# Attention states stored by strips of two heads, late results in the attention weights' banks, dense operands moved to 128 bytes past a multiple of 512

## The chip, the cores and the metric

The kernel runs on one core of one Trainium2 chip. The metric is the device time in microseconds of one execution. Three executions of the kernel before took 1625.15, 1625.56 and 1628.57 us, median 1625.56.

## The reference

The input is x, 8 rows of 512 tokens of 512 numbers, float32. Cut to what matters:

```python
xn = layernorm(x)                                  # no weights
# attention layer s(xn): a gated recurrence over tokens, 16 heads, keys of 16, values of 32
a  = rmsnorm(xn, ln1_w)
q, k, v, g = a @ Wq, a @ Wk * 32**-0.5, a @ Wv, a @ Wg + bg
gk = log_sigmoid(a @ Wkg1 @ Wkg2 + bkg2) / 16      # rank 16 inside
S  = S * exp(gk_t)[..., None] + k_t[..., None] * v_t[..., None, :]   # per head, 16 x 32
o_t = q_t @ S
o  = silu(g) * normalised_per_head(o)
x1 = xn + o @ Wo
s  = x1 + (silu(rmsnorm(x1, ln2_w) @ W1) * (rmsnorm(x1, ln2_w) @ W3)) @ W2   # hidden 1408
# the other branch: 8 low-rank experts mixed by a softmax, rank 64
g2 = silu(sum_k alpha_k * U_k @ (V_k @ xn)),  alpha = softmax(relu(xn @ fW1 + b1) @ fW2 + b2)
out = x + s * g2
```

## The kernel before

Every large product is made in float32r from operands split into a high and a low part: three matmuls (hi·hi, hi·lo or lo·hi, and the third) into one PSUM bank (`product3`, lines 153 to 163). A plain float32 matmul shows as two records in the trace.

There are three stages, one after the other, each a loop over the 8 rows (counted from 0 here): `phase_f` (names f_, the layer norm, the experts and the gate), `phase_a` (names a_, attention) and `phase_m` (names m_, the MLP and the output). At each seam work of the next stage is put into the last row of the one before: `Lent` gives attention's first keys, queries and gates banks of the f stage, and `Front` in `phase_m` gives the MLP's first three hidden blocks (of 128) the dense banks of attention's last row.

The order of the work is written out by hand for each engine (`sync`, `vector`, `gpsimd`, `scalar`, `tensor` in each stage), with semaphores counted through `Counts`. `loop_parts` runs a body per row and, inside it, named parts of the row ahead. A class `Regions` is a ring of PSUM places: results take them in turn in a fixed order, and `free`, `ready` and `taken` are the waits for a place empty, filled and read.

A row of attention, on PE: for each of 4 chunks of 128 tokens, the masked attention weights within the chunk (`weights`, L1282: 64 products on 32x32 tiles, heads' pairs on four strips of 32 partitions, each strip in a bank of its own), the turned keys (L1366, two transposes), a part of the next row (k0 and k1, the inner gate u, q0, q1), the variance of the chunk before (L1303), the product of the carried state with the queries (L1390), the state's addition (`state_products`, L1351) and the weighted values (L1399, 16 heads, 128x32 tiles). Then the key gates z, the values v0 to v3, the output gates g0 to g3 and the output products o0 to o3. The state has for each of two groups of 8 heads 128 partitions (8 heads of 16 keys) by 256 columns (8 heads of 32 values), with zeros outside each head's block, made on DVE with `hmask` (L1031) and decayed on L1043. ACT reads the mix (L1216 square, L1219 copy, after DVE's L1063 of the chunk before), the turned keys (L1203), q and k (L1129), and v (L1149). The inner gate is copied on DVE in four steps (L931 to L935). DVE clears the attention weights' banks once (`clear_weights`, L1012), since the upper halves of blocks are never written.

Of the 8 banks attention has four `a_ps` (three for the dense ring, one for the mix) and four for the attention weights. An MLP row is 11 blocks: `up_products` (L1529 to L1531, 2 x 12 matmuls, stationary operand m_w, moving m_xs) and `down` (L1543 to L1545, 12 matmuls, moving m_h). Block j uses tile m_w`j`.

Tensors in SBUF stand in the order of their allocation, each rounded up to 32 bytes. In the built program the constants begin at byte 16512 of a partition and row0 at 19136. Counting on from there: a_wkhi to a_wolo begin 192 past a multiple of 512, all dense tensors of the f stage and a_xa begin 128 past one, a_og and a_v_tok 192, m_w0 to m_w4 192 (they take the place of the attention weights), m_w5 to m_w10, m_xs and m_h 128.

## Time and profile before

| | |
|---|---|
| median of 3 runs | 1625.56 us (1625.15 to 1628.57) |
| the profiled execution | 1622.4 us |
| its span, first to last instruction | 1620.7 us |
| mean granted clock of TensorE | 0.998 |
| PE busy | 1593.2 us, 98% |
| PE weight loads | 1277.6 us, 79% |
| DVE, ACT, POOL busy | 847.3, 567.2, 167.2 us |

The f stage ends at about 342 us, attention at 885 us, the MLP fills the rest. Busy time is that of the union of an engine's records. A matmul's record reaches from its start to its modelled end, over the start of the next, so neither the busy share of PE nor a matmul's mean says how fast matmuls follow each other. The start of one stretch in the timeline and the start of the next do.

### The profile page before, as it was taken

The numbers are of one execution on the slowest core, as the hardware profiler recorded it, in microseconds if no ns is written. First come the engines' busy times: TensorE is split into PE (matmuls) and PEld (weight loads), VectorE is DVE, ScalarE is ACT, GpSimd is POOL, SyncE is SP. The second block draws the span as 40 slices with busy tenths as digits, with TensorE's granted clock in tenths as the row PEclk, the third lists the DMA queues.
The fourth block names the chain that finished last, engine by engine and source line by source line (L and its number), as shares of the span: only waits on it lengthen the run. The fifth ranks groups of instructions, "written<-read, shape, count | busy, mean of one in ns | idle before, by whom it ended". The sixth has DMA issues, their size and how long they took to land.

```text
span 1620.7 us, 30581 instructions
## 1 busy us (share of the span) xinstructions
PE 1593.2 (98%) x12274; PEld 1277.6 (79%) x12274; DVE 847.3 (52%) x1311; ACT 567.2 (35%) x982; POOL 167.2 (10%) x190
## 2 busy tenths in 40 slices
PE   7999999999999999999999999999999999999998
PEld 5777888777777777777777788888888888888886
DVE  5565455367797887978876451331415142241413
ACT  4333343366564645636564411111111111111111
POOL 4770000100220102101020000000000000000000
PEclk9999999999999999999999999999999999999999
DMA  7563332101020210202213423030301203030200
GB/s 175 151 135 78 83 95 69 59 27 52 9 84 0 84 53 32 84 0 84 84 54 118 144 101 127 0 136 0 136 0 49 87 0 136 0 136 0 91 14 26
DMA packets 50700, 113.16 MB, mean 70 GB/s; under 512 B 13321, under 2 KB 24665, under 8 KB 42466
## 3 DMA queue, kind: packets, MB, share of 16 engines
q1 hardware_dynamic: 47906, 99.95, 19.5%
q10 hardware_dynamic: 1152, 8.39, 1.3%
q0 software_dynamic: 1600, 4.25, 0.9%
q8 instruction: 28, 0.46, 0.1%
q14 instruction: 14, 0.11, 0.0%
HBM read 78.98 MB, written 33.59 MB: 69 GB/s over the span
## 4 chain that ended last, share of the span: by engine, by line
PE 94%; DVE 2%; ACT 1%; issue 1%; DMA 1%; PEld 0%; SPq 0%; ACTq 0%; DVEq 0%; PEldq 0%
PE m_ps L1529 10%; PE m_ps L1531 10%; PE m_ps L1530 10%; PE a_ps L160 7%; PE a_ps L162 7%; PE a_ps L161 7%; PE f_ps L160 5%; PE f_ps L162 5%; PE f_ps L161 5%; PE m_ps L1543 5%; PE m_ps L1544 5%; PE m_ps L1545 5%; PE a_att L1282 3%; PE a_ps L1399 2%; PE a_ps L1303 2%; PE a_ps L1390 1%
## 5 line engine op out<-in xcount | busy, mean ns | idle before, releaser
L1529 PE MATMUL m_ps<-m_xshi,m_w 128*128 128x512 f32 x680 | 268.1, 394 | 1.4 <-DVE m_w L1520 1.4
L1766 DVE TENSOR_TENSOR m_h<-m_ps,m_silu 128x512 f32<-128x512 f32 x85 | 58.7, 690 | 402.4 <-PE m_ps L1531 402.4
L1531 PE MATMUL m_ps<-m_xshi,m_w 128*128 128x512 f32 x680 | 266.5, 392 | 0.0
L1530 PE MATMUL m_ps<-m_xslo,m_w 128*128 128x512 f32 x680 | 266.4, 392 | 0.0
L1830 ACT ACTIVATE m_silu<-m_ps 128x512 f32<-128x512 f32 x85 | 50.8, 597 | 334.3 <-PE m_ps L1531 334.3
L1529 PEld LDWEIGHTS m_ps<-m_xshi,m_w 128*128 128x128 f32 x680 | 127.7, 188 | 30.0 <-issue 2.1
L1531 PEld LDWEIGHTS m_ps<-m_xshi,m_w 128*128 128x128 f32 x680 | 127.6, 188 | 28.7
L1530 PEld LDWEIGHTS m_ps<-m_xslo,m_w 128*128 128x128 f32 x680 | 127.7, 188 | 28.1 <-issue 0.2
L1101 POOL TENSOR_TENSOR row<-row,a_r 128x512 f32<-128x512 f32 x32 | 50.7, 1615 | 331.6 <-DMA a_r<-scratch_r 331.6
L1022 DVE TENSOR_TENSOR a_a<-a_att,causal 128x1024 f32<-128x1024 f32 x64 | 75.2, 1216 | 11.8 <-PE a_att L1282 11.8
L1839 ACT ACTIVATE m_h0hi<-m_h 128x512 fp32r<-128x512 f32 x46 | 29.1, 632 | 135.7 <-DVE m_h L1766 135.7
L1543 PE MATMUL m_ps<-m_h0hi,m_w 128*128 128x512 f32 x192 | 75.3, 392 | 0.0
L1544 PE MATMUL m_ps<-m_h0lo,m_w 128*128 128x512 f32 x192 | 75.3, 392 | 0.0
L1545 PE MATMUL m_ps<-m_h0hi,m_w 128*128 128x512 f32 x192 | 75.3, 392 | 0.0
L1839 ACT ACTIVATE m_h1hi<-m_h 128x512 fp32r<-128x512 f32 x39 | 24.7, 632 | 115.6 <-DVE m_h L1766 115.6
L1107 POOL TENSOR_TENSOR a_cum<-a_cum 128x512 f32<-128x512 f32 x24 | 30.7, 1281 | 321.3 <-ACT a_cum L1190 321.3
L1543 PE MATMUL m_ps<-m_h1hi,m_w 128*128 128x512 f32 x160 | 62.6, 391 | 0.0
L1544 PE MATMUL m_ps<-m_h1lo,m_w 128*128 128x512 f32 x160 | 62.6, 391 | 0.0
L1545 PE MATMUL m_ps<-m_h1hi,m_w 128*128 128x512 f32 x160 | 62.6, 391 | 0.0
L160 PE MATMUL f_ps<-f_xnhi,f_w1hi 128*128 128x512 f32 x128 | 52.1, 407 | 2.5 <-DVE f_xnlo L476 1.2
L160 PE MATMUL a_ps<-a_wvhi,a_xahi 128*128 128x512 f32 x128 | 53.1, 415 | 0.0
L160 PE MATMUL a_ps<-a_xahi,a_wghi 128*128 128x512 f32 x128 | 50.8, 397 | 0.9 <-ACT a_v_tok L1149 0.6
(306 smaller groups left out, 3487.9 us busy)
## 6 DMA issues: line engine op xcount, KB each, us to landing
row<-scratch_xn SPq DMA_DIRECT2D x16, 1024.0 KB, 4.9
row<-scratch_xmid SPq DMA_DIRECT2D x16, 1024.0 KB, 7.3
m_xt<-in_L_attn_W SPq DMA_DIRECT2D x33, 256.0 KB, 3.2
f_xt<-in_L_attn_x SPq DMA_DIRECT2D x32, 256.0 KB, 8.1
scratch_xn<-row SPq DMA_DIRECT2D x8, 1024.0 KB, 9.0
scratch_gate<-row ACTq DMA_DIRECT2D x8, 1024.0 KB, 3.9
scratch_xmid<-row SPq DMA_DIRECT2D x8, 1024.0 KB, 3.9
row<-scratch_gate SPq DMA_DIRECT2D x8, 1024.0 KB, 10.5
```

Source lines behind the costliest of these rows:

```text
L160: pe.matmul(out, lh, rh, start=first and n == 0, stop=False)
L161: pe.matmul(out, lh, rl, start=False, stop=False)
L162: ins = pe.matmul(out, ll, rh, start=False, stop=last and n == end)
L1022: dve.tensor_tensor(a_sb[n].rearrange("p s g o t -> p (s g o) t"), ps, bcast(causal, 1, 4 * GR), ALU.mult).then_inc(att.taken_sem(f"{c}_{n ...
L1529: pe.matmul(ps, wh, xh, start=k == 0, stop=False)
L1530: pe.matmul(ps, wh, xl, start=False, stop=False)
L1531: ins = pe.matmul(ps, wl, xh, start=False, stop=k == LAST)
L1543: pe.matmul(ps, lh, rh, start=j == 0, stop=False)
L1544: pe.matmul(ps, lh, rl, start=False, stop=False)
L1545: ins = pe.matmul(ps, ll, rh, start=False, stop=j == FT - 1)
L1766: dve.tensor_tensor(h[n], dense.region(f"b{j}"), silu[n], ALU.mult).then_inc(dense.taken_sem(f"b{j}"), 1)
L1839: act.activation(h_hl[n][0], h[n], ACT.Copy).then_inc(count.sem("hhi"), 1)
```

## The change

- States: 128 partitions by 2 x 32 columns per group (a partition holds its head's values in one of two column halves, chosen by `parity`), not 256. One DVE operation makes both groups. The product with the queries is made by strips of 32 partitions (two heads), 64 output partitions each, eight per chunk.
- PSUM: two dense banks, two for the mix (even and odd quads of heads), and the attention weights' four banks take z0, z1, v1, v2, g0, g1, g2 as well. Places are given by a table in place of turns. The turned keys go to the second half of the mix's odd bank. `clear_weights` goes.
- Inner gate: the weights hold its 16 columns three times high and once low, so one ACT copy of 64 partitions and one DVE subtraction fill what four DVE operations did. Its matmuls have 64 and 48 columns in place of 48 and 16.
- SBUF: small tensors and a pad of 256 bytes go ahead of the attention weights, a pad of 448 bytes ahead of m_w0; decay and last stand behind a_v_tok.

The diff, cut to its core:

```diff
     def __init__(self, counts, name, regions, order, early=(), places=None):
...
-            r = n % len(regions)
+            r = places[result] if places else n % len(regions)
...
+    w = {name: sb(name, shape) for name, shape in (
+        ("bkg2", [P, KD // P]), ("bg", [P, KT]), ("ln1", [P, KT]), ("mean", [P, D // 32]),
+        ("ln2", [P, KT]), ("pad", [P, 64]))}
...
-    w["wkg1"] = sb("wkg1", [P, KT, 32 + RANK], F32R)
+    w["wkg1"] = sb("wkg1", [P, KT, 4 * RANK], F32R)
...
-        state = [sb(f"state{n}", [P, GR, HG * VH]) for n in range(2)]
+        state = [sb(f"state{n}", [P, GR, 2 * VH]) for n in range(2)]
...
-        psum = [ctx.enter_context(nc.psum_tensor(f"a_ps{b}", [P, 512], F32))[:] for b in range(4)]
+        psum = [ctx.enter_context(nc.psum_tensor(f"a_ps{b}", [P, 512], F32))[:] for b in range(2)]
+        ps_mix = ctx.enter_context(nc.psum_tensor("a_mix", [P, 2, 512], F32))[:]
+        EVEN, ODD = 0, 1
...
+        places = {result: n for n, results in enumerate((
+            ["k0", "ds0", "var0", "q0", "ds2", "var2", "var3", "v3", "o0", "o2"],
+            ["k1", "u", "ds1", "var1", "q1", "ms", "v0", "g3", "o1", "o3"],
+            ["z0", "g0"], ["z1", "g1"], ["v1", "g2"], ["v2"])) for result in results}
...
+        turned = Regions(count, "kt", [ps_mix[:, ODD, GR * P:]], list(range(NC - 1)))
-        mix = Regions(count, "mix", psum[3:4], list(range(NC)))
+        mix = Regions(count, "mix", [ps_mix[:, :, 0:QD // 2 * P]], list(range(NC)))
...
 # DVE, inner gate
-                dve.tensor_copy(u[0:RANK], ps).then_inc(count.sem("uhi"), 1)
-                dve.tensor_copy(u[64:64 + RANK], ps).then_inc(count.sem("uhi"), 1)
-                dve.tensor_copy(u[96:96 + RANK], at.region("u")[32:32 + RANK]).then_inc(count.sem("uhi"), 1)
                 dve.wait_ge(*count.at("uhi", i))
-                dve.tensor_tensor(u[32:32 + RANK], ps, u[0:RANK].bitcast(F32), ALU.subtract).then_inc(at.taken_sem("u"), 1)
+                dve.tensor_tensor(u[low], at.region("u")[low], u[low].bitcast(F32), ALU.subtract).then_inc(at.taken_sem("u"), 1)
 # DVE, state
-                        for g in range(GR):
-                            ins = dve.tensor_tensor(new[:, g, :].rearrange("p (h o v) -> p h o v", o=2, v=VH),
-                                                    bcast(ds[:, g], 1, HG // 2),
-                                                    bcast(hmask.rearrange("p (h o) -> p h o", o=2), 3, VH), ALU.mult)
+                        dve.tensor_tensor(new.rearrange("p g (o v) -> p g o v", v=VH), ds,
+                                          bcast(bcast(parity, 1, GR), 3, VH), ALU.mult).then_inc(dense.taken_sem(f"ds{c}"), 1)
 # ACT
+            def inner_gate(i, at=dense):
+                act.wait_ge(*at.ready("u", i))
+                act.activation(u[0:4 * RANK], at.region("u")[0:4 * RANK], ACT.Copy).then_inc(count.sem("uhi"), 1)
...
+                    if c == 0:
+                        keys(i, c)
+                    if c == 1:
+                        squares(i, (2,))
+                    for part in (("k0", "k1"), ("u",), ("q0",), ("q1",))[c]:
                         ahead(part)
+                    if 0 < c < NC - 1:
+                        keys(i, c)
 # PE
+                    for part in (("k0", "k1"), ("u",), ("q0",), ("q1",))[c]:
+                        ahead(part)
+                    if 0 < c < NC - 1:
+                        pe.wait_ge(*mix.taken(c - 1, i))
+                        turned_keys(i, c)
...
+                    if 0 < c < NC - 1:
+                        pe.wait_ge(*turned.taken(c, i))
...
-                        for quad in range(QD):
-                            g, first_head = quad * HQ // HG, quad * HQ % HG
-                            pe.matmul(ps[:, quad, :], state[c % 2][:, g, first_head * VH:(first_head + HQ) * VH],
-                                      qhat[:, gcs[g], :], start=quad == 0, stop=True, skip_group_check=True)
+                        for g in range(GR):
+                            for strip in range(4):
+                                rows, at = slice(H32 * strip, H32 * (strip + 1)), H64 * (strip % 2)
+                                pe.matmul(ps[2 * g + strip // 2][at:at + H64], state[c % 2][rows, g, :],
+                                          qhat[rows, gcs[g], :], start=g == 0, stop=True, skip_group_check=True,
+                                          tile_position=(H32 * strip, at))
...
+            parts["v0"](0)
+            for m in range(KT):
+                pe.wait_ge(*f.dense.taken(f"u{m}", NB - 1))
+            for part in ("v1", "g"):
                 parts[part](0)
+            pe.wait_ge(*dense.taken(f"g{LAST - 1}", 0))
...
+        sb("pad", [P, 112])
         w = [sb(f"w{j}", [P, 3, 2, KT, P], F32R) for j in range(5)]
```

## Rows read from the trace of the kernel before

**Rows 1.** the profile page, its head, busy times and clock in 40 slices.

```profile
span 1620.7 us, 30581 instructions
...
PE 1593.2 (98%) x12274; PEld 1277.6 (79%) x12274; DVE 847.3 (52%) x1311; ACT 567.2 (35%) x982; POOL 167.2 (10%) x190
...
PEclk9999999999999999999999999999999999999999
```

**Rows 2.** the list of what PE waited for: engine, line, releaser: us, times, longest.

```profile
PE a_ps L160 <- DVE a_xalo L923: 1.6, 1, 1.6
PE m_ps L1529 <- DVE m_w L1520: 1.4, 1, 1.4
```

**Rows 3.** timeline of PE, MLP row 1: start us, us, engine, line, out<-in, count.

```profile
983.29 0.40 PE L1529 MATMUL m_ps<-m_xshi,m_w 128*128 128x512 f32 x1
...
988.89 0.40 PE L1543 MATMUL m_ps<-m_h0hi,m_w 128*128 128x512 f32 x1
...
1024.71 0.39 PE L1529 MATMUL m_ps<-m_xshi,m_w 128*128 128x512 f32 x1
...
1030.15 0.39 PE L1543 MATMUL m_ps<-m_h1hi,m_w 128*128 128x512 f32 x1
```

**Rows 4.** timeline of PE, first and next-after matmul of four stretches of 48.

```profile
331.44 0.39 PE L160 MATMUL f_ps<-f_vxhi,f_uthi 128*128 128x512 f32 x1
...
342.33 0.40 PE L160 MATMUL a_ps<-a_wvhi,a_xahi 128*128 128x512 f32 x1
...
353.34 0.39 PE L160 MATMUL a_ps<-a_xahi,a_wghi 128*128 128x512 f32 x1
...
478.81 0.39 PE L160 MATMUL a_ps<-a_xahi,a_wghi 128*128 128x512 f32 x1
...
490.00 0.40 PE L160 MATMUL a_ps<-a_oghi,a_wohi 128*128 128x512 f32 x1
...
500.68 0.39 PE L162 MATMUL a_ps<-a_oghi,a_wolo 128*128 128x512 f32 x1
```

**Rows 5.** timeline of PE, attention row 2, chunk 1.

```profile
514.44 1.05 PE L1390 MATMUL a_ps<-a_neg,a_state 128*128 128x128 f32 x8
...
515.43 0.43 PE L1351 MATMUL a_ps<-a_v_tok,a_fold 128*32 128x64 f32 x16
...
515.67 0.52 PE L1399 MATMUL a_ps<-a_a,a_v_tok 128*32 128x128 f32 x12
...
516.66 0.33 PE L1282 MATMUL a_att<-a_qx,a_lv 32*32 32x128 f32 x6
...
518.29 0.33 PE L1366 MATMUL a_ps<-ident,a_soft 128*128 128x128 f32 x1
```

**Rows 6.** timeline of DVE, the same chunk; in brackets idle time before.

```profile
513.80 0.67 DVE L931 CAST a_u<-a_ps 16x512 fp32r<-16x512 f32 x1
...
516.64 0.76 DVE L1031 TENSOR_TENSOR a_state<-a_ps,hmask 128x256 f32<-128x256 f32 x2
...
518.50 0.69 DVE L1063 TENSOR_TENSOR a_rn<-a_rn,a_oc 128x512 f32<-128x512 f32 x1
```

**Rows 7.** timeline of attention row 0: PE's gates and outputs, DVE's last weighing.

```profile
411.33 0.50 PE L160 MATMUL a_ps<-a_xahi,a_wghi 128*128 128x512 f32 x1 [0.48 <-ACT a_v_tok L1149]
...
423.60 0.39 PE L160 MATMUL a_ps<-a_oghi,a_wohi 128*128 128x512 f32 x1
...
424.87 1.22 DVE L994 TENSOR_TENSOR a_neg<-a_neg,a_q 128x1024 f32<-128x1024 f32 x1
```

**Rows 8.** timeline of attention row 2, chunk 2: ACT, and PE's start of the variance.

```profile
519.23 0.60 ACT L1219 ACTIVATE a_oc<-a_ps 128x512 f32<-128x512 f32 x1 [1.83 <-DVE a_rn L1063]
...
519.72 0.38 ACT L1203 ACTIVATE a_fold<-a_ps 128x256 f32<-128x256 f32 x1
...
521.36 0.59 PE L1303 MATMUL a_ps<-a_sq,avg 128*128 128x512 f32 x1
...
521.56 0.60 ACT L1129 ACTIVATE a_q<-a_ps 128x512 f32<-128x512 f32 x1 [1.45 <-PE a_ps L162]
```

More of the change, by code:

```diff
@@ L269, in prepare_attention_weights @@
     step(pool.memset(w["wkg2"].bitcast(F32), 0.0))
-    step(pool.memset(w["wkg1"].bitcast(F32), 0.0))
     RANK, KD = Wkg2.shape
-    small = w["stage"][0:RANK, 1, 0:KD]
+    small = w["stage"][0:4 * RANK, 1, 0:KD]
     sources = {"wkg1": Wkg1, "wk": Wk, "wq": Wq, "wv": Wv, "wg": Wg, "wo": Wo}
@@ L795, in phase_a @@
         wkg1, wq, wk, wv, wg, wo = (w[name] for name in ("wkg1", "wq", "wk", "wv", "wg", "wo"))
-        RANK = wkg1.shape[2] - 32
+        RANK = wkg1.shape[2] // 4
         wkg2, bkg2_sb, bg_sb, ln1_sb = w["wkg2"], w["bkg2"], w["bg"], w["ln1"]
@@ L836, in phase_a @@
                           ("decay", 1), ("m64", 3), ("m32", 3), ("mdk", 1), ("mdq", 2), ("mkh", 1), ("mqh", 1),
-                          ("state", GR * (NC - 2)), ("first", NC - 1), ("weighing", NC),
+                          ("state", GR * (NC - 2)), ("weighing", NC),
                           ("sq", NC), ("rn", NC), ("og", 2 * NC), ("oghi", NC), ("oglo", NC)):
@@ L843, in phase_a @@
         assert GR == 2 and NC == 4
[L845 to L848 removed]
+        order = [("k0", ["k0"]), ("k1", ["k1"]), (None, ["ds0"]), ("u", ["u"]), (None, ["var0", "ds1"]),
+                 ("q0", ["q0"]), (None, ["var1", "ds2"]), ("q1", ["q1"]), (None, ["var2", "ms"]),
+                 ("z", zs), ("v0", values[:1]), (None, ["var3"]), ("v1", values[1:]), ("g", gates),
                  (None, outs), ("body", [])]
+        places = {result: n for n, results in enumerate((
+            ["k0", "ds0", "var0", "q0", "ds2", "var2", "var3", "v3", "o0", "o2"],
+            ["k1", "u", "ds1", "var1", "q1", "ms", "v0", "g3", "o1", "o3"],
+            ["z0", "g0"], ["z1", "g1"], ["v1", "g2"], ["v2"])) for result in results}
         early = {part: results for part, results in order if part}
[L851 to L852 removed]
+        dense = Regions(count, "dense", psum + [ps[:, strip].rearrange("p g o t -> p (g o t)") for ps in ps_att for strip in range(2)],
+                        sum((results for _, results in order), []), sum(early.values(), []), places)
+        turned = Regions(count, "kt", [ps_mix[:, ODD, GR * P:]], list(range(NC - 1)))
         att = Regions(count, "att", ps_att, [f"{c}_{n}" for c in range(NC) for n in range(2)])
[L854 removed]
+        mix = Regions(count, "mix", [ps_mix[:, :, 0:QD // 2 * P]], list(range(NC)))
         LAST = KT - 1
@@ L1005, in clear @@
                 dve.memset(u.bitcast(F32), 0.0)
-            def clear_weights():
-                for m in range(KT):
-                    dve.wait_ge(*f.dense.taken(f"u{m}", NB - 1))
-                for ps in ps_att:
-                    for strip in range(2):
-                        dve.memset(ps[:, strip], 0.0)
             def body(i, ahead):
@@ L1196, in deviation, with keys, by_quads @@
                 act.activation(added[0:1], added[0:1], ACT.Exp, scale=-0.5).then_inc(count.sem("r2"), 1)
+            def keys(i, c):
+                act.wait_ge(*turned.ready(c, i))
+                act.activation(flat(kt_sb), turned.region(c), ACT.Copy).then_inc(turned.taken_sem(c), 1)
+            def by_quads(ap):
+                return ap.rearrange("p (g b) t -> p g b t", b=2)
             def body(i, ahead):
@@ L1245, in first_row @@
                 elif part == "lent":
-                    for name in ("k0", "k1"):
+                    for name in ("u", "k0", "k1"):
                         parts[name](0, first)
@@ L1317, in inner_gate @@
                 for k in range(KT):
-                    pe.matmul(ps[0:32 + RANK], wkg1[:, k, :], xa_hl[0][:, k, :], start=k == 0, stop=False,
+                    pe.matmul(ps[0:4 * RANK], wkg1[:, k, :], xa_hl[0][:, k, :], start=k == 0, stop=False,
                               skip_group_check=True)
-                    ins = pe.matmul(ps[0:RANK], wkg1[:, k, 0:RANK], xa_hl[1][:, k, :], start=False, stop=k == LAST,
+                    ins = pe.matmul(ps[0:3 * RANK], wkg1[:, k, 0:3 * RANK], xa_hl[1][:, k, :], start=False, stop=k == LAST,
                                     skip_group_check=True)
@@ L1379, in body @@
                     pe.wait_ge(*mix.free(c, i))
-                    ps = mix.region(c).rearrange("p (q t) -> p q t", t=P)
+                    ps = [mix.region(c)[:, (EVEN, ODD)[quad % 2], quad // 2 * P:(quad // 2 + 1) * P] for quad in range(QD)]
+                    if 0 < c < NC - 1:
+                        pe.wait_ge(*turned.taken(c, i))
                     if c > 0:
@@ L1561, in gpsimd @@
             def gpsimd(pool):
-                zs, (v0,), (_, v2, v3), (g0, g1, g2, g3) = (a.early[part] for part in ("z", "v0", "v1", "g"))
-                pass_over(pool, a.dense, zs + [v0, v2, v3, g1, g2, g0, g3], NB)
+                pass_over(pool, a.dense, ["v3", f"g{LAST}"], NB)
             @staticmethod
@@ L1663, in second_and_third @@
                     hidden(1, "q0")
-                    hidden(2, "v1")
+                    hidden(2, "v0")
                     lo(1)
```

96 lines of the change are left out of this document (39 added, 57 removed).

## The prediction

> **What bounds the kernel now.** I read the page first. The span is 1620.7 us, PE is busy in 98% of it at a granted clock of nine tenths or more in every slice (the 2.4 GHz level), DVE in 52%, ACT in 35% and POOL in 10% [rows 1]. The list of what PE waited for adds up to little: 1.6 us for the first attention row's keys (their operand's chain starts at the gate products before them, which the change leaves) and 1.4 us for weights of the MLP [rows 2]. So a change pays only if PE's instructions follow each other faster. The busy time and the mean of a matmul (389 to 394 ns) don't show that, because the records overlap: a matmul starts while the one before it drains. The measure I use is the spacing of starts in the timeline.
>
> In the MLP stage two stretches of the same line, 24 matmuls each over one weight tile, differ: 983.29 to 988.89, 5.60 us or 233.3 ns per matmul, and 1024.71 to 1030.15, 5.44 us or 226.7 ns [rows 3]. The first reads its weights from m_w3, the second from m_w8. The moving operand (m_xs) is the same. By the order of allocation m_w0 to m_w4 begin 192 bytes past a multiple of 512, while m_w5 to m_w10 and m_xs begin 128 past one. In the attention stage the gate products (weights a_wg at 192, moving a_xa at 128) take 11.19 us for 48, 233.1 ns each. The output products (a_wo at 192, moving a_og at 192) take 10.68 us for 47 spacings, 227.2 ns. The f_vx, f_ut products of the first stage (both at 128) take 10.89 us for 48, 226.9 ns. The value products (stationary a_xa at 128, moving a_wv at 192) take 11.01 us for 48, 229.4 ns [rows 4]. So the slow spacing goes with operands whose start differs modulo 512, in both stages, and equal starts run at about 227.
>
> **Part 1, the starts.** The small tensors and a pad go ahead of the attention weights: five tensors, rounded up to 32 bytes 192 in all, plus 256 bytes of pad make 448, and 192 + 448 = 640 is 128 past 512. The m_w0 to m_w4 tiles get the same through a pad of 448. The wider wkg1 and the strip-sized states keep what follows at 128 too. Every dense operand then stands as f_vx, f_ut do now, so I take 226.7 ns. MLP: weight tiles 0 to 4 have 24 up and 12 down matmuls each, 180 per row, 1440 in all; times 6.6 ns is 9.5 us. Attention: keys, queries and gates are 24 + 24 + 48 per row, 768 in eight rows, times 6.6 ns, 5.1 us. Values: 384 times 2.7 ns, 1.0 us. The inner gate's 64: 0.3 us. Together 15.9 us. One piece is given back: in the first MLP row PE waits 1.4 us for DVE's weight parts [rows 2], which hang on loads and not on PE, and the 60 faster matmuls just ahead of it would only lengthen that wait by 0.4 us. **Gain 15.5 us.** Bounds: nothing (next paragraph) and 16.5 us, if the values come down by 6.6 ns as well.
>
> On the spacing, the trace is silent about why equal starts help. The Trainium skill (SBUF — State Buffer, section A bandwidth-pool intuition that's wrong) gives TensorE two independent read ports, one for the moving operand and one for LDWEIGHTS. By that rule the start of one against the other could not matter, and part 1 would be worth nothing. The pair of rows above speaks against it; it is rival B below.
>
> **Part 2, the states by strips.** For chunks 1 to 3 PE now makes four products of 128 rows by 128 columns: eight records in 0.99 us (514.44 to 515.43) [rows 5], so 0.25 us per product, of which 0.1 is the change of tile shape on leaving (the eight starts are 0.112 apart, 0.90 in all). It becomes eight products of 32 rows by 64 columns, four strips at a time. What four tiles at a time cost is seen in the weighted values: 16 products of 128 columns on four column tiles take 0.99 us (515.67 to 516.66) [rows 5], or, less 0.1 for the shape, 0.22 us per round of four. That rows of tiles also run side by side is seen in the attention weights: 64 small products with 5120 moving columns end in 1.63 us (516.66 to 518.29) [rows 5]; at 0.247 us per 128 columns one after another they would need 9.9 us, so six run at once. So two rounds are 0.44 us, and the shape now changes twice (0.1 on entry after the variance product, 0.1 on leaving): 0.64 us. 24 chunks times (0.99 - 0.64) is **a gain of 8.4 us**. Bounds: no price for the shape, 24 x 0.55 = 13.2 us; the strips one after another in pairs, four rounds, 0.88 + 0.2 = 1.08 us, a loss of 2.2 us. I stand near the first, since six at once is what the nearest row shows.
>
> On DVE the two state copies (0.76 us) become one of 128 columns in place of twice 256, the decays shrink from 256 to 64 columns, and of the four inner gate steps, 0.67 us for the first and as much for the others, three go; ACT gets one copy in their place, about as long as its query copy, 0.60 us [rows 6, 8]. That is over 2 us of air for DVE in chunk 1. PE waits for none of it now, so it is worth nothing by itself.
>
> **Part 3, results in the attention weights' banks.** Late results (z, v1, v2, g0 to g2) no longer share three banks. In the body of row 0 ACT is late with the exponentials and PE waits for banks: 0.48 us before the first gate product, and the 48 gate matmuls take 12.27 us against 11.19 us a row later [rows 4, 7]. That is 1.6 us, and no other row shows it. I take **1.5 us** and not all, because the output products now have two banks, and the third of them needs DVE's first addition. DVE's weighing ends at 426.09, the addition takes 0.7 us, so 426.8; PE would reach the third product 24 matmuls after 423.60 less 1.6, 0.3 (gates) and 0.1 (values): 427.0 [rows 7].
>
> **Part 4, new waits.** The turned keys now share a bank with the mix. In chunks 1 and 2 their transposes come after the inner gate or query product, and wait for ACT's copy of the mix before. That copy ended at 519.83 where PE would come at 521.4, 1.5 us later, so this is hidden [rows 8]. Then PE may not start the state products until ACT has copied the keys (0.38 us). ACT is in order and has the query (or inner gate) copy ahead of it: 0.20 us after PE's next start, for 0.60 [rows 8]. So the keys are out 1.08 us after the dense product, plus 0.06 to tell PE, against 0.19 (transposes) + 0.86 (variance) = 1.05 without a wait. 0.1 us, 16 times: 1.6 us lost. The mean square product now needs the last query's bank: copied 0.80 us after, needed at 0.86, so nothing. In the last row the MLP's product in v0's bank waits for ACT's deviation, which does not come sooner, so one chunk's 0.35 us is given back, 0.4 rounded. **Loss 2.0 us.** Bounds: nothing, and 0.6 us per stop (the ACT copy wholly uncovered), 9.6 us.
>
> **The rest.** DVE's four memsets of the weights' banks go, and PE gets waits for the first stage's last results and for g2: both in the stretch where PE works through 11 us each of values and gates [rows 4], with the copies it waits for one result or more behind. In the first stage's last row the inner gate's copy moves into ACT's queue ahead of the key copies: PE's one stall there is for DVE's products with alpha, which wait for ACT's alpha copies, and these come after the second key copy in either version. Nothing. POOL's three more small loads and changed copies run beside the first stage, at 10% of the span [rows 1], and are needed at its end. Nothing.
>
> **Sum.** 15.5 + 8.4 + 1.5 - 2.0 = 23.4 us. The profiled execution took 1622.4 us (span 1620.7 and 1.7 around it), so it would take 1599.0. Its time lies 3.2 us under the median of the runs, 1625.56, and against that median the forecast is **1602.2 us**.
>
> **Rivals.**
> A, strips that don't run together (chance 0.10). Strips 0 and 1 write the same bank, at different partitions; in the attention weights each of the four strips has a bank of its own, so no row shows this case. Against it: four column tiles of the weighted values write one bank together. If pairs queue up, part 2 loses 2.2 us instead of gaining 8.4: 1612.8 us. The Trainium skill (TensorEngine Tiling (Array Packing), section Gotcha 1: PSUM Pressure) says that different row tiles cannot access the same PSUM bank simultaneously and software must keep them apart; by that rule this would be the case that comes true, or worse. No row here shows it.
> B, the starts don't matter (0.10): the slow spacing belongs to something else that goes with those tiles, so part 1 gives nothing: 1617.7 us. For it: only a correlation. Against it: it holds over two stages, and the 192/192 pair is fast.
> C, both A and B (0.03): 23.4 - 15.5 - 10.6 = -2.7, 1628.3 us, within 0.2%, which is about what a measurement of this kernel can tell from no change. It is also where the change does not do what it says.
> D, slower (0.03): the stop of part 4. PE at the transposes hangs on ACT's mix copy, that on DVE's multiplication before it. If the 1.5 us of air is gone, a stop costs the multiplication, the mix copy, the query copy and the keys copy, 0.69 + 0.60 + 0.60 + 0.38 = 2.3 us [rows 6, 8], 16 times, 36 us; less 25.4 us of gains that is 11 us slower, 1637 us. It decides from 1.6 us per stop. Against it: DVE gets shorter in just that stretch.
> The forecast has 0.74.
>
> **Range.** Down: part 2 at 13.2 and no new wait would give 1595; I end at 1597. Up: it takes in A and a part of the stops, 1614. B, C and D lie outside with 0.16. Faster by over 0.2%: 0.94 (forecast, A, B); within: 0.03 (C); slower: 0.03 (D).
>
> **What the profile will show.** Right: up products over m_w0 to m_w4 in 5.44 us per 24, gates in 10.9 us per 48, the state records of a chunk in 0.6 to 0.7 us, the gates in row 0's body as short as those of the next, PE between the variance and the states idle for 0.1 us or less. Wrong: 5.60 us again (B), 1.0 us or more for the states (A), PE waits for ACT's a_fold or a_oc copies in tens of us (D).

## The result, and the profile after

The changed kernel takes 1613.08 us (median of four runs, 1610.89 to 1615.69) where the kernel before took 1626.14 beside it: a ratio of 0.9918, 95% interval 0.9899 to 0.9937, so 10 to 16 us faster. The forecast of 23.4 us was too large by some 10. The profiled execution took 1612.38 us, its span is 1610.6, 10.1 less than before [rows 1].

The page of the changed kernel: head, busy times, clock, and the queue that brings instructions (packets, MB, share).

```profile
span 1610.6 us, 30883 instructions
...
PE 1574.2 (98%) x12466; PEld 1262.7 (78%) x12466; DVE 817.5 (51%) x1259; ACT 572.4 (36%) x990; POOL 164.9 (10%) x191
...
PEclk9999999999999999999999999999999999999999
...
q8 instruction: 29, 0.48, 0.1%
```

What PE waited for: engine, line, releaser: us in total, times, longest.

```profile
PE a_att L1295 <- issue: 6.5, 6, 2.1
...
PE f_ps L696 <- DVE f_xt L470: 1.4, 1, 1.4
...
PE m_ps L1918 <- DVE row L1818: 1.1, 6, 0.2
...
PE a_mix L1412 <- issue: 0.4, 1, 0.4
```

The row of a_att is the news: "issue" is time in which PE waited for nothing that the profile shows, and before it was 1.4 us in two stops on the same products. The length of a stop is given below as this list has it, idle time alone.

**Where the time went.** A row's or a stage's length is read from the starts of its first matmuls. Timeline of PE in the kernel before: the first query product, the output products of rows 6 and 7, the first turn of MLP rows 0 and 1, and the last turn.

```profile
325.73 0.50 PE L160 MATMUL f_ps<-a_xahi,a_wqhi 128*128 128x512 f32 x1 [1.07 <-DVE row L530]
...
822.00 0.40 PE L160 MATMUL a_ps<-a_oghi,a_wohi 128*128 128x512 f32 x1
...
874.09 0.50 PE L160 MATMUL a_ps<-a_oghi,a_wohi 128*128 128x512 f32 x1
...
964.60 0.27 PE L1891 MATMUL m_ps<-ident,row 128*128 128x128 f32 x1
...
1057.51 0.27 PE L1891 MATMUL m_ps<-ident,row 128*128 128x128 f32 x1
...
1613.07 0.30 PE L1900 MATMUL m_ps<-ident,row 128*128 128x128 f32 x1 [3.02 <-DVE row L1789]
```

The same in the changed kernel, with the output products of rows 0 and 1 as well (before: 423.60 and 490.00, [rows 7, 4]).

```profile
328.44 0.50 PE L161 MATMUL f_ps<-a_xahi,a_wqhi 128*128 128x512 f32 x1 [1.07 <-DVE row L535]
...
425.15 0.39 PE L161 MATMUL a_ps<-a_oghi,a_wohi 128*128 128x512 f32 x1
...
490.18 0.39 PE L161 MATMUL a_ps<-a_oghi,a_wohi 128*128 128x512 f32 x1
...
815.31 0.39 PE L161 MATMUL a_ps<-a_oghi,a_wohi 128*128 128x512 f32 x1
...
872.20 0.50 PE L161 MATMUL a_ps<-a_oghi,a_wohi 128*128 128x512 f32 x1
...
962.28 0.27 PE L1918 MATMUL m_ps<-ident,row 128*128 128x128 f32 x1
...
1054.16 0.27 PE L1918 MATMUL m_ps<-ident,row 128*128 128x128 f32 x1
...
1603.72 0.30 PE L1927 MATMUL m_ps<-ident,row 128*128 128x128 f32 x1 [3.03 <-DVE row L1816]
```

| stretch, us | before | after | difference | forecast's steps |
|---|---|---|---|---|
| start to first query product | 325.73 | 328.44 | +2.7 | 0 |
| to output products of row 0 | 97.87 | 96.71 | -1.2 | -3.8 |
| rows 1 to 6 (before 66.40 a row, after 65.03) | 398.40 | 390.16 | -8.2 | -10.0 |
| last row | 52.09 | 56.89 | **+4.8** | -1.0 |
| to the first MLP turn | 90.51 | 90.08 | -0.4 | -0.4 |
| MLP rows to the last turn | 648.47 | 641.44 | -7.0 | -8.3 |
| rest of the span | 7.6 | 6.9 | -0.7 | 0 |

The forecast's column is the prediction's own steps shared out: a steady attention row 0.82 (96 matmuls of 6.6 ns, 48 of 2.7, 8 of 6.6) and 1.05 for the states less 0.2 for waits, 1.67; an MLP row 180 times 6.6 ns, 1.19; row 0 takes 1.5 for the banks and 0.6 for its own first products besides. So the two loops, attention rows 1 to 6 and the MLP rows, did four fifths of what was forecast (15.2 of 18.3 us). Two things are not forecast at all: the last attention row is 4.8 us longer, and the first stage 2.7, which the change hardly touches. The way to the outputs of row 0 is also 2.6 us short of its forecast.

**Part 1 in the rows.** Timeline of PE, MLP row 1, the 24 up products over m_w3, first and next-after matmul:

```profile
980.72 0.39 PE L1558 MATMUL m_ps<-m_xshi,m_w 128*128 128x512 f32 x1
...
986.16 0.39 PE L1572 MATMUL m_ps<-m_h0hi,m_w 128*128 128x512 f32 x1
```

5.44 us, 226.7 ns each, where it was 5.60 [rows 3]. In this MLP row every whole stretch of up or down products, over each of the eleven tiles, now follows at 226.7 ns; only the 24 up products that the turns cut in two take longer, 5.67 us.

**Part 2 in the rows.** Attention row 2, chunk 1: turned keys, variance, states, state products.

```profile
513.48 0.38 PE L1373 MATMUL a_mix<-ident,a_soft 128*128 128x128 f32 x2
513.70 1.02 PE L1316 MATMUL a_ps<-a_sq,avg 128*128 128x512 f32 x2
514.65 0.67 PE L1412 MATMUL a_mix<-a_neg,a_state 32*64 32x128 f32 x16
515.25 0.43 PE L1364 MATMUL a_ps<-a_v_tok,a_fold 128*32 128x64 f32 x16
```

The states take 0.60 us (514.65 to 515.25) against 0.99 [rows 5]: the strips run together. The first four of their records start within 0.02 us of each other and last 0.32 us each. The turned keys take 0.22 (before 0.19) and the variance 0.95 (before 0.86): part of the entry price and of the new waits stands there. By such starts, one whole middle row, in us, with two kernels of the experiments beside it:

| group of PE | before | after | e4 (full states) | e3 (before, equal starts) |
|---|---|---|---|---|
| keys, queries, inner gate (56) | 13.50 | 13.29 | 13.30 | 13.35 |
| values, gates, outputs (144) | 33.62 | 33.20 | 33.18 | 33.43 |
| turned keys, three times | 0.57 | 0.67 | 0.67 | 0.57 |
| variance 1 to 3, mean square | 3.44 | 3.80 | 3.65 | 3.44 |
| states, three chunks | 2.94 | **1.80** | 3.13 | 2.95 |
| row | 66.40 | 65.03 | 66.15 | 66.07 |

**The last row.** Timeline of PE in the third set of attention weights (idle before, and its releaser, in brackets):

```profile
845.92 0.34 PE L1295 MATMUL a_att<-a_qxd,a_dk 32*32 32x64 f32 x13
848.34 0.43 PE L1295 MATMUL a_att<-a_qxd,a_dk 32*32 32x64 f32 x7 [2.08 <-issue]
848.71 0.80 PE L1558 MATMUL a_ps<-m_xshi,m_w 128*128 128x512 f32 x1
...
850.15 0.63 PE L1558 MATMUL a_ps<-m_xshi,m_w 128*128 128x512 f32 x1
```

PE stops in the middle of small products that all its semaphores allow. The windows view of the stretch behind it gives (us, PE, PEld, DVE, ACT, POOL busy, granted clock, DMA share, GB/s):

```profile
848.00:851.40 3.40, 3.06 (x13) 2.34 (x13) 2.35 (x2) 0.00 (x0) 0.00 (x0) 0.50 0.00 0
```

The clock is at its lower level, 1.2 GHz, for 3.4 us right after PE stood still for 2.1: by an estimate from that half speed another 1.7 us. The DMA view has the instruction queue (q8) between 822 and 874 us:

```profile
q8 instruction: 8, 0.13, 0.9%
```

One of these 16 KB packets begins at 846.0, just ahead of the stop. Between 430 and 820 us, where the loop runs, that view has none. The row has four such stops.

### The profile page after: what moved, and what is told of

Same layout as the page of the kernel before. It is cut to its first block, busy times and chain, and to the rows that moved or that the text cites. A ratio compares the mean times of both kernels' runs of the same rounds, so it can differ in the third digit from the quotient of the medians.

```text
span 1610.6 us, 30883 instructions
## 1 busy us (share of the span) xinstructions
PE 1574.2 (98%) x12466; PEld 1262.7 (78%) x12466; DVE 817.5 (51%) x1259; ACT 572.4 (36%) x990; POOL 164.9 (10%) x191
## 4 chain that ended last, share of the span: by engine, by line
PE 89%; DVE 6%; issue 1%; DMA 1%; ACT 1%; SPq 1%; DVEq 0%; PEld 0%; ACTq 0%; PEldq 0%; POOLq 0%
PE m_ps L1558 9%; PE m_ps L1560 9%; PE m_ps L1559 9%; PE f_ps L161 5%; PE f_ps L163 5%; PE f_ps L162 5%; PE a_ps L161 5%; PE a_ps L163 5%; PE a_ps L162 5%; PE m_ps L1573 4%; PE m_ps L1574 4%; PE m_ps L1572 4%; PE a_att L1295 3%; PE a_att L163 2%; PE a_att L161 2%; PE a_att L162 2%
## 5 line engine op out<-in xcount | busy, mean ns | idle before, releaser
L1098 POOL TENSOR_TENSOR row<-row,a_r 128x512 f32<-128x512 f32 x32 | 51.6, 1641 | 331.3 <-DMA a_r<-scratch_r 331.3
L1295 PE MATMUL a_att<-a_qxd,a_dk 32*32 32x64 f32 x2048 | 49.6, 225 | 3.7 <-issue 3.7
L161 PE MATMUL f_ps<-f_xnhi,f_vthi 128*128 128x512 f32 x128 | 51.6, 403 | 0.0
```

What stands on the lines that cost most here:

```text
L161: pe.matmul(out, lh, rh, start=first and n == 0, stop=False)
L1295: return pe.matmul(ps[s:s + H32, strip % 2, g, :, at:at + q.shape[2]], keys[rows, g * NC + c, s:s + H32], q[rows], start=True, stop=True, ...
```

## Experiments

The theory to test first: part 1 works by starts that are alike; parts 2 and 4 do what the table says; the missing time is lost where PE's instructions are fetched. Rivals: chance from execution to execution, a wait or an operation of the last row, some property of 128. The runs are told in four groups.

**The changed kernel again (e1).** No edit.

> The changed kernel once more, unaltered, for what a second look shows of two losses that the prediction did not have. In the first look the attention stage began 2.6 us later than before (344.9 against 342.3 us), and in attention's last row PE stood still on small L1295 matmuls for 1.08, 1.17 and 2.29 us with nothing to wait for, followed by 3.4 us at the lower of the two clock levels. Theory 1 (instruction supply): those stops come from where 16 KB packets of PE's instruction queue fall in the code, so they stand at the same places again, within 0.3 us each, and the last row again takes 56.9 us from output product to output product where before took 52.1. Theory 2 (chance): the stops move or go, the last row takes 50 to 53 us, and the late start shrinks below 1 us. Time by either: 1610 to 1616 us.

1612.63 us, ratio 0.9919 (0.9903 to 0.9935), span 1608.3. Waits of PE:

```profile
PE a_att L1295 <- issue: 7.2, 6, 2.4
```

The last row takes 56.7 us, with stops at the same four places to the instruction. One is 0.5 us longer, which is more than the 0.3 that the expectation allowed, and two are 0.3 longer: 5.6 us in all where the first profile had 4.5. The clock did not fall this time, so a stop of 2.1 to 2.4 us doesn't always bring that. The first query product came at 325.88, as before the change. In the 14 profiles of this case, whose first stages do the same matmuls, it came between 324.5 and 332.5: the 2.7 us at the start are chance. Theory 1 holds for the places of the stops in the last row (their lengths vary), theory 2 for the first stage.

**Parts undone, or done alone (e2, e3, e4).** e2 puts the starts back:

```diff
-    w = {name: sb(name, shape) for name, shape in ( ... ("pad", [P, 64]))}
-    w.update({name: [sb(name + part, [P, KT, n], F32R) ...
+    w = {name: [sb(name + part, [P, KT, n], F32R) ...
...
-        sb("pad", [P, 112])
```

> The changed kernel with its starts put back (attention weights and the first five MLP weight tiles at 192 bytes past a multiple of 512 again), so parts 2 to 4 alone. Theory 1 (the starts are worth what the spacing of matmuls says): MLP row 92.9 to 93.0 us again, 1.0 us longer than in the changed kernel, attention row about 66.0, 1.0 us longer; 14 to 16 us slower than the changed kernel, that is 1627 to 1630, no faster than before. Theory 2 (by the prediction's steps as they stood): parts 2 to 4 give 7.9 us by themselves, 1618. The rival that something else sped the dense matmuls up: within 3 us of the changed kernel.

1627.47 us, ratio 1.0008 (0.9996 to 1.0021): parts 2 to 4 alone are worth nothing that can be measured. It is 14.8 us slower than e1. Two output products one row apart:

```profile
490.52 0.39 PE L161 MATMUL a_ps<-a_oghi,a_wohi 128*128 128x512 f32 x1
...
556.39 0.40 PE L161 MATMUL a_ps<-a_oghi,a_wohi 128*128 128x512 f32 x1
```

65.87 us a row: 0.84 more than with the starts. 0.32 of that is new: in this kernel the gated output stands at 128 and its weights at 192, and the 48 output products take 11.29 us where the changed kernel has 10.97 and before had 11.00 (490.00 to 501.00; [rows 4] shows 47 of the 48 spacings). A pair of equal starts was turned into an unequal one, and slowed down. Over eight rows that is 2.6 of the 14.8 us, so e2 puts the starts, against those of the kernel before, nearer 12 us. Against before (66.40) the row is 0.53 shorter, from parts 2 and 4 together, and would be 0.82 shorter without those output products.

e3 is the kernel before with everything moved up to 192:

```diff
-                        ("ln2", [P, KT]), ("stage", [P, 2, D])):
+                        ("ln2", [P, KT]), ("pad", [P, 16]), ("stage", [P, 2, D])):
```

(and decay and last behind v_tok, in place of ahead of it).

> The kernel before with one pad of 64 bytes ahead of the staging buffer, and two small tiles moved behind the last large one: activations, MLP tiles 5 to 10 and the gated output then start at 192 past a multiple of 512, as the attention weights and the first five MLP tiles do already. Nothing stands at 128 any more. Theory 1 (what counts is that both operands start alike modulo 512): MLP matmuls over tiles 0 to 4 at 226.7 ns, gates at about 227, 15 us faster than before: about 1611 us, and faster than the changed kernel if its parts 2 to 4 are worth nothing. Theory 2 (128 is what helps): all tiles run at 233 ns, MLP weight tiles 5 to 10 among them, 11 us slower than before. Theory 3 (the starts don't matter): no change, 1626.

1614.34 us, ratio 0.9925 (0.9909 to 0.9942), 11 us faster from 64 bytes of padding, and within its interval as fast as the whole change. MLP up products take 5.44 us per 24 with both operands at 192. It is alike starts that count, not 128. The output products around the last attention row:

```profile
822.62 0.39 PE L160 MATMUL a_ps<-a_oghi,a_wohi 128*128 128x512 f32 x1
...
874.22 0.50 PE L160 MATMUL a_ps<-a_oghi,a_wohi 128*128 128x512 f32 x1
```

The middle rows take 66.07, longer by 1.04 than after; but the last row 51.6, shorter by 5.3. Most of what parts 2 to 4 gain in six rows (6.2 us) is given back in one.

e4 is the changed kernel with full products for the states:

```diff
-        state = [sb(f"state{n}", [P, GR, 2 * VH]) for n in range(2)]
+        state = [sb(f"state{n}", [P, GR, HG * VH]) for n in range(2)]
...
-                                pe.matmul(ps[2 * g + strip // 2][at:at + H64], state[c % 2][rows, g, :], ...
+                            pe.matmul(ps[quad], state[c % 2][:, g, ...], qhat[:, gcs[g], :], ...
```

> The changed kernel with part 2 undone: four state products of 128 rows by 128 columns per chunk again, and the state tiles back at their old size (which moves every dense start from 128 to 384, all still alike). Theory 1 (the strips are worth their row): state products 0.98 us per chunk against 0.60, less 0.1 that the change of tile shape on entry cost, 0.28 x 24 = 6.7 us slower, 1619 to 1621. Theory 2 (strips are worth little, because the variance and mean square products around them got longer by 2 and 1.5 us): 3 to 5 us slower. Instruction supply: PE has 24 matmuls fewer per row here, so the stops of the last row stand elsewhere, and up to 5 us may come back with them; the period of the middle rows, where the code is in place, leaves them out and is read first: 65.1 us against 65.1 + 0.8 by theory 1, + 0.4 to 0.6 by theory 2.

1617.20 us, ratio 0.9946 (0.9931 to 0.9962), 4.6 us slower than e1. Row 2, chunk 1:

```profile
511.33 1.02 PE L1319 MATMUL a_ps<-a_sq,avg 128*128 128x512 f32 x2
512.22 1.16 PE L1413 MATMUL a_mix<-a_neg,a_state 128*128 128x128 f32 x8
513.31 0.43 PE L1367 MATMUL a_ps<-a_v_tok,a_fold 128*32 128x64 f32 x16
```

The states take 1.09 us here, the row 66.15: the strips are worth 1.12 us a row, more than theory 1 had. The full products are 0.10 longer than the same products before the change (0.99 [rows 5]). The likely cause is the wait for the turned keys' copy, which this kernel has too: chunk 3, the one without that wait, takes 0.98. All dense operands stand at 384 here, and the up products run at 226.7 ns. Its last row takes 56.4 us, with the packet edges nearly where before had them (instructions 141 and 653 against 147 and 659), but with a third stop of 1.7 us at 1421, a wait of 0.6 before the states, and 3.4 us at the lower clock. So the loss in the last row does not come from the strips: it is there without them. That leaves PE's order and waits of parts 3 and 4, which no run took apart.

**Where instructions are fetched (e5, e6, e7, e9, e10).** Each is the changed kernel with so many semaphore increments spread over PE's value and gate products ahead of the attention loop:

```diff
+            filler, left = outer.enter_context(nc.semaphore("a_filler")), [34, 32]
...
+                    for _ in range(n):
+                        pe.sem_inc(filler, 1)
```

> The changed kernel with 34 semaphore increments added to PE's program, two at a time between the long value and gate products ahead of the attention loop, where each has 0.7 us of matmuls to hide in. Nothing else changes, but all of PE's later code moves by 34 instructions. In the two looks at the changed kernel the last attention row stopped at its instructions 93, 605, 1117 and 1373, counted from the loop's exit: whole multiples of 256 apart, and PE's instruction queue brings 16 KB packets, 256 instructions of 64 bytes. Theory 1 (instruction supply by such packets): the candidates move to 59, 571, 827, 1083 and 1339. 59 lies behind 37 long matmuls, whose 4 us cover a fetch of 2.3 us, so that stop goes; the others lie in small matmuls and stay: the last row 55 to 56 us instead of 56.8, 1 us faster in all. Theory 2 (the stops belong to a wait or an operation of the row): they stay at 93, 605, 1117, 1373 and the row at 56.8 us; plus at most 0.5 us for the increments.

1612.50 us, ratio 0.9912 (0.9895 to 0.9928). The stops moved with the code, from 93, 605 and 1117, counted from the branch at the loop's exit, to 59, 571 and 1083. Theory 1 of two: they belong to places of the program, multiples of 256 instructions apart, not to an operation. But 59 still costs 1.4 us, and one at 315 costs 0.4 in the middle of long matmuls: that these cover a fetch was wrong. The one forecast at 1339 did not come, and PE now waits 0.9 us for DVE's multiplication of the attention weights, which it didn't before. Last row 56.3 us, and no gain in all; from the first query product to the last row's outputs it takes 541.8 us, where the changed kernel took 543.8 and 543.2 in its two profiles.

> The same with 128 increments. Theory 1: candidates at 221, 477, 733, 989, 1245 and 1501 of the last row; 733 lies behind long matmuls, the others in or right behind small ones: three or four stops, row 55 to 58 us. Theory 2: stops at 93, 605, 1117, 1373 as before, 56.8 us, plus up to 2 us if 128 increments don't hide.

> The same with 202 increments, which puts the packets' borders where the kernel before has them in the last row: 147, 403, 659, 915, 1171, 1427. Before, only 147 and 659 stopped it, for 0.55 and 1.02 us, and the row took 52.1 us. Theory 1: stops at 147 and 659 again, perhaps at 1427; the row 53 to 54 us, 3 us faster than the changed kernel, less what the increments cost, about 1610 us. Theory 2: 56.8 us and the stops where they were.

1636.41 us (1.0067, 1.0045 to 1.0089) and 1630.49 us (1.0014, 1.0001 to 1.0027): 24 and 18 us slower than the changed kernel, which neither theory had. The last rows are short, 55.3 and 55.6. The middle rows aren't: 67.9 to 72.0 us with 128 increments, 66.3 to 68.4 with 202. The instruction queue brought 84 and 85 packets where it brought 29, nine more in each pass of the loop, and PE's waits list has 17 and 10 stops in small products. Inside the loop the stops come back in every pass at the same places, counted in the trace from the loop's branch: 653 and 1421, three times 256 apart, with 128 increments, and 1090 with 202. The loop had stopped being kept. With 202 the last row has its stops at 659 and 1427 and none at 147, and is not the 53 to 54 us that theory 1 gave.

> The changed kernel with 48 increments. What the runs with 34, 128 and 202 left open: with 0 and 34 PE's instruction queue brings nothing between the first and the last pass of the attention loop, with 128 and 202 it brings eight 16 KB packets in every pass, which costs 1 to 7 us per row. Counted from the program, a pass has 1980 instructions of PE. If the core keeps eight packets of 256 (2048), the loop stays in place only while it begins no later than instruction 68 of a packet; by where the stops of the last row lie it begins at 9, so at 57 with 48 increments. Theory 1 (eight packets stay, counted from a packet's edge): 57 + 1980 = 2037, the loop stays in place, rows of 65.0 us. The last row's edges come to 45, 557, 813, 1069 and 1325: 45 lies right behind long matmuls. Row 55 to 57 us, 1611 to 1614 in all. Rival (the refetching came from the increments' number or their sitting in the code, growing with it): some rows already longer than 65.5 us.

> The same with 72 increments: the loop begins at 81 of a packet, and 81 + 1980 = 2061 is past 2048. Theory 1: eight packets or more in every pass, rows of 66 to 70 us in place of 65.0, 1620 to 1640 us in all, from 24 increments more than in the run with 48. Rival (the cost grows smoothly with the increments): between the runs with 48 and 128, at most 1 us per row.

1613.10 us (0.9939, 0.9916 to 0.9961) and 1635.01 us (1.0069, 1.0052 to 1.0086). The pages of the two, and two output products one row apart in each, e9 first:

```profile
q8 instruction: 29, 0.48, 0.1%
```

```profile
487.68 0.39 PE L161 MATMUL a_ps<-a_oghi,a_wohi 128*128 128x512 f32 x1
...
552.62 0.39 PE L161 MATMUL a_ps<-a_oghi,a_wohi 128*128 128x512 f32 x1
```

and e10:

```profile
q8 instruction: 84, 1.38, 0.3%
```

```profile
492.00 0.39 PE L161 MATMUL a_ps<-a_oghi,a_wohi 128*128 128x512 f32 x1
...
560.04 0.39 PE L161 MATMUL a_ps<-a_oghi,a_wohi 128*128 128x512 f32 x1
```

with, in the waits of that pass of e10 (492 to 560 us):

```profile
PE a_att L1295 <- issue: 2.2, 2, 1.3
```

24 increments more, and every pass fetches its code again, nine packets of 16 KB: 64.94 us becomes 68.04. So the cliff lies between 48 and 72 increments, where the expectation had put it, but with nine packets a pass and not the eight that I had expected. The count behind it, a loop that begins at instruction 9 of a packet and may end at 2048 at most, is not shown. If the stops stand exactly at the packets' edges, the one 93 instructions behind the exit puts the changed kernel's loop of 1980 at 231 of a packet, which is nine packets and yet kept, and e10's at 47, which is eight and yet fetched. The count holds only if the edges lie 28 to 45 instructions ahead of the stops (the expectation has 34 without saying so), and no run measures that. What fell with e9 is the guess on single stops: the edges at 45 and 301 cost 0.9 and 1.4 us, and its last row, 59.3 us with another 3.4 us at the lower clock, is the longest of all.

**The size of a difference (e8), and ACT's order (e11, e12).** e8 starts the MLP tiles 0 to 4 32, 64, 128, 256 and 384 bytes away from their activations:

```diff
-        sb("pad", [P, 112])
-        w = [sb(f"w{j}", [P, 3, 2, KT, P], F32R) for j in range(5)]
+        w = []
+        for j, room in enumerate((120, 8, 16, 32, 32)):
+            sb(f"pad{j}", [P, room])
+            w.append(sb(f"w{j}", [P, 3, 2, KT, P], F32R))
```

> The changed kernel with other pads ahead of the first five MLP weight tiles, so that they start 32, 64, 128, 256 and 384 bytes (tiles 0 to 4) past the residue of the activations they meet, modulo 512; tiles 5 to 10 stay alike. Per 24 up matmuls equal starts take 5.44 us, and starts 64 apart took 5.60. Theory 1 (any difference of start modulo 512 costs the same 6.6 ns): all five tiles 5.60 us; the MLP row 93.0 us, 8 us slower than the changed kernel. Theory 2 (the cost goes with a smaller period, 64 or 128 bytes): tiles 2 to 4 at 5.44, tile 0 or tiles 0 and 1 at 5.60; 2 to 4 us slower. Theory 3 (the cost grows with the distance): unequal steps, the largest for 256.

1622.74 us, ratio 0.9976 (0.9964 to 0.9988), MLP row 92.70. The 12 down products over tiles 2, 3 and 4, first and next-after matmul of each:

```profile
989.77 0.40 PE L1574 MATMUL m_ps<-m_h0hi,m_w 128*128 128x512 f32 x1
992.57 0.39 PE L1560 MATMUL m_ps<-m_xshi,m_w 128*128 128x512 f32 x1
...
998.14 0.39 PE L1574 MATMUL m_ps<-m_h1hi,m_w 128*128 128x512 f32 x1
1000.86 0.39 PE L1560 MATMUL m_ps<-m_xshi,m_w 128*128 128x512 f32 x1
...
1006.31 0.40 PE L1574 MATMUL m_ps<-m_h0hi,m_w 128*128 128x512 f32 x1
1009.10 0.40 PE L1560 MATMUL m_ps<-m_xshi,m_w 128*128 128x512 f32 x1
```

2.80, 2.72 and 2.79 us: 233 ns each with a difference of 128 bytes, 227 with 256, 233 with 384. The down products over tiles 0 and 1 (32 and 64) run at 233 as well. None of the three theories: a difference of 256 costs nothing and the others nearly the same, so what counts is the start modulo 256, as far as five differences can say.

e11 lets ACT copy the turned keys of chunks 1 and 2 of the last row ahead of the MLP's piece:

```diff
+                    early = isinstance(i, int) and 0 < c < NC - 1
+                    if early:
+                        keys(i, c)
                     for part in (("k0", "k1"), ("u",), ("q0",), ("q1",))[c]:
                         ahead(part)
-                    if 0 < c < NC - 1:
+                    if 0 < c < NC - 1 and not early:
```

> The changed kernel with ACT's order altered in the last attention row alone: in chunks 1 and 2 it copies the turned keys before it does the MLP's piece (a silu copy of 0.60 us and two weight copies) rather than behind it. Every look at the changed kernel had PE wait 0.61 us between variance and states there, for that copy, and PE's program is the same to the instruction. Theory 1 (only the copy is late): that 0.61 us goes, the other stops stay where they were within 0.3 us: 0.6 us faster, row 56.2 us, 1612 us in all. Theory 2 (a wait there also holds up the fetch of the next packet): the stop at instruction 1373 (0.84 us, twice) goes or shrinks below 0.4 us as well: 1.2 to 1.5 us, row 55.3 to 55.6. Rival (the MLP's pieces are now late on ACT): up products wait for m_w or a bank, no gain or slower.

1614.86 us, ratio 0.9915 (0.9898 to 0.9931). PE at the variance and the states:

```profile
854.45 1.02 PE L1319 MATMUL a_ps<-a_sq,avg 128*128 128x512 f32 x2
855.40 0.67 PE L1415 MATMUL a_mix<-a_neg,a_state 32*64 32x128 f32 x16
```

0.95 us from one to the other, as in the middle rows, where it was 1.47 (853.04 to 854.51): the wait for ACT, 0.5 us, is gone. The stop at 1373 stays at 0.75, so that wait did not hold it up, and in chunk 3 PE now waits 1.1 us for DVE's multiplication of the attention weights (as in e5 and e9, 0.9 and 0.8 us). The row is 57.6 us: no gain. e12 adds the 34 increments.

> The same with the 34 increments as well, which gave the shortest first pass of the loop (97.1 against 98.0 us) and a last row of 56.3 us. If both add up: last row 55.0 to 55.7 us, 1611 us, the shortest attention stage of the kernels with the change, by 1.5 us or so against the changed kernel, which three rounds may not tell apart from it (0.1%).

1611.09 us, ratio 0.9885 (0.9868 to 0.9903), the lowest ratio of all, but its interval overlaps the changed kernel's, its last row is 56.1, not 55.0 to 55.7, and its attention stage as a whole is no shorter. I don't count it as better.

## Why the prediction was right and wrong

The prediction had the direction, and both of its main mechanisms work as described: alike starts and strips that run together. That the range holds the result is luck. The upper end, 1614, was set by rival A and a part of the stops of part 4, and neither happened; what moved the time there, 0.9 us short of that end, is not in the prediction. By the time alone the result would be rival A's (1612.8). Of the rows that the prediction named as signs, those of part 1 and part 2 came as said, 5.44 us per 24 up products, 10.88 per 48 gates and 0.60 for the states. By its own steps:

**Part 1, 15.5 us: right in kind, somewhat oversized.** Rival B falls: e3 shows the gain with the starts alone changed, and e2 loses it. So what the prediction drew from the Trainium skill (SBUF — State Buffer, section A bandwidth-pool intuition that's wrong), that with two independent read ports the start of one operand against the other could not matter, does not hold here; why it matters stays open. The spacing came down to 226.7 ns as said. What came short: an MLP row gave 1.03 us in place of 1.19, as PE now waits 0.2 us for DVE's part of the turns (1.1 us in six waits, not there before), and the first five or six products of a group of keys or queries still follow at 228 to 236 ns. An attention row gave 0.63 (first two lines of the row table) in place of 0.82. In all some 13 us. One limit of my reading: I took the starts modulo 512 from a correlation in which only one difference, 64 bytes, occurred, and e8 shows that 256 counts as alike.

**Part 2, 8.4 us: right.** 0.60 us a chunk plus 0.05 on entry (0.15 a row, after against e4), forecast 0.64 with the entry in it; e4 puts it at 1.12 us a row, forecast 1.05. Rival A falls: strips 0 and 1 write one bank at different partitions and do run together, in 0.60 us where rival A had 1.08. The Trainium skill's rule (TensorEngine Tiling (Array Packing), section Gotcha 1: PSUM Pressure), that different row tiles cannot access the same PSUM bank simultaneously, does not hold here in that wide form, as the states' 0.60 us show; strips that share partitions and bank were not run.

**Part 3, 1.5 us: not seen in the time.** The first pass gave 1.2 to 1.4 us in place of 3.8, and it has two stops by instruction supply of 0.8 to 1.2 us. The gates of row 0 follow one another without ACT's 0.48 us, so the wait did go, but its sum was lost in the same pass.

**Part 4, 2.0 us lost: about 3.** The row table has 0.10 us for the turned keys' transposes, and 0.36 for the variances and mean square, of which 0.15 goes with the tile shape (after against e4) and the rest with waits. That leaves 0.3 us a row where 0.2 was forecast. In the last row the states start 0.61 us later behind the variance than before the change. Rival D's chain of 2.3 us per stop occurred nowhere.

**"The rest: nothing" is the step that failed.** I costed PE's moved and added instructions by what they execute, and left out that they have to be brought. The last row, straight code behind the loop, was forecast 1.0 us shorter and became 4.8 longer, and the first pass lost about 2.5, of which its two stops are 1.6 to 2.0. The stops of the last row are 4.5 us by the waits list against 1.4 before, the lower clock added 1.7 in the profiled execution, and the wait before the states 0.6: 5.4 of the 5.8 us by which that row missed. In e1 the same row missed by 5.6 with 5.6 us of stops, the same wait and no lower clock: 4.8 us. With some 2.5 in the first pass, 2.5 of part 1 and 1 of part 4 that is 11 to 12 us, about the 10 that lie between 23.4 and 13; single profiles don't tell it closer. The packet edges were there to be seen before: 28 packets in the page's queue list, and 1.4 us of "issue" in two stops on small products. What brings the loss is shown for the place of the code (e5) and for the loop that no longer fits (e9, e10). That parts 3 and 4 rather than the strips bring most of the last row's is inferred from one comparison (e3 with e4), and what in them does is not shown. Why the edge at 1421 stops PE in e4 and the one at 1427 didn't before, and what in the code makes a fetch begin, stays open; the stops of the last row end 2.2 to 2.9 us after a packet begins, in every profile here.

## What to carry to other kernels

Look at the spacing of like matmuls before rearranging work: 64 bytes of padding gave most of this change's gain, and a pad that makes one pair of operands alike can make another unlike. Count the instructions of the busiest engine's loop and watch the instruction queue on the page: if packets come in every pass (nine here), a harmless edit has pushed the loop past what is kept. Code that runs once behind a loop and consists of small matmuls pays for its fetches, so a gain per row must be set against the first pass and the last.

## What the runs showed of the hardware

- PE's instructions come in packets of 16 KB over a queue of their own (q8). Its stops stand multiples of 256 instructions apart (93, 605, 1117, 1373) and move with the code. A stop in the small products cost 0.3 (e3) to 2.4 us (e9), one in long matmuls 0.4 (e5) to 2.0 (e10), and those of the last row ended 2.2 to 2.9 us after a packet began.
- A loop of 1980 PE instructions by the program (1968 of them are in the trace) is kept with 0, 34 and 48 increments ahead of it and fetched anew in every pass with 72, 128 and 202. With 72 that costs 3 to 5 us per pass of 65, 22 us in all. The changed kernel thus has between 48 and 71 instructions to spare.
- Products of 512 columns on fp32r operands follow at 226.7 ns with starts alike modulo 256 (both at 128, 192 or 384) and at about 233 ns with differences of 32, 64, 128 and 384 bytes (e8, and 64 in the kernel before); that 256 is the period rests on these five. With the activations stationary and the weights moving, the value products, the same difference of 64 cost 2.7 ns [rows 4] instead of 6.6; why is open.
- After stops of 1.6 to 2.4 us the granted clock fell to its lower level for 3.4 us in some executions and not in others: e1 against the first profile, the same program, and e11, where it fell at 371.6 us behind a wait of 1.6 us that nearly every profile has.
